# All three expert weights split in two, w_down multiplied by eighteen fp32r products: attention with a mixture of experts behind it, on one core

## The reference

```
x = layernorm(x + attn(x, bv_q, bv_k, bv_v))
    Q = sign(x * sign(bv_q)); K = sign(x * sign(bv_k)); V = x * sign(bv_v)
    attn = sum over s <= t of sigmoid(4 * Q.K / 16) * V        (causal)
x = layernorm(x + ffn(x, w_router, w_gate, w_up, w_down))
    top1 = argmax(softmax(x @ w_router)); 32 experts, 320 places each, in order of arrival
    g = buf @ w_gate[e]; u = buf @ w_up[e]                     (320 x 256, 256 x 256)
    y = (silu(g) * u) @ w_down[e]                              (320 x 256, 256 x 256)
    out = x + y * gate   for rows that got a place, else x
```

## Time and profile before

| | us |
|---|---|
| median of 3 runs | 582.45 |
| lowest, highest | 579.06, 582.63 |
| the profiled execution | 580.2 |
| its span | 578.5 |
| TensorE busy | 544.3 |
| VectorE busy | 386.5 |
| ScalarE busy | 356.0 |
| POOL busy | 380.7 |

### The profile page before, as it was taken

The page is one execution under the profiler, slowest core; times in us unless marked ns, Lnnn a source line. Parts: engine busy times, 40 slices in busy tenths (PEclk is TensorE's granted clock), DMA queues, the critical chain, the costliest instruction groups (busy, mean ns, idle before and its releaser), DMA issues.

```text
span 578.5 us, 11994 instructions
## 1 busy us (share of the span) xinstructions
PE 544.3 (94%) x3953; PEld 465.2 (80%) x3953; DVE 386.5 (67%) x986; ACT 356.0 (62%) x707; POOL 380.7 (66%) x547
## 2 busy tenths in 40 slices
PE   5999999999999999999998999999999999999960
PEld 4889898898888989889895388888888888888840
DVE  2765877957787669777664447667777777777730
ACT  5786977959778596877871135555555555555530
POOL 3547887688776878777753505666666666666663
PEclk9999999999999999999998899999999999999995
DMA  8994233243322443117410146666666666665300
GB/s 245 370 336 141 80 104 89 83 141 94 93 56 87 144 94 119 46 37 207 166 58 7 60 125 194 198 196 193 193 196 185 184 188 190 197 192 180 113 21 34
DMA packets 80637, 81.47 MB, mean 141 GB/s; under 512 B 20362, under 2 KB 71802, under 8 KB 80576
## 3 DMA queue, kind: packets, MB, share of 16 engines
q1 hardware_dynamic: 73664, 66.41, 38.9%
q0 software_dynamic: 6912, 14.30, 6.9%
HBM read 44.29 MB, written 37.90 MB: 142 GB/s over the span
## 4 chain that ended last, share of the span: by engine, by line
PE 84%; DVE 5%; issue 3%; DMA 2%; POOL 2%; ACT 1%; SPq 0%; DVEq 0%; POOLq 0%; ACTq 0%
PE ps L1004 15%; PE ps L838 10%; PE ps L839 10%; PE ps L840 10%; PE ps L816 9%; PE ps L982 8%; PE ps L990 6%; PE ps L983 6%; PE ps L960 2%; PE ps L857 2%; DVE hl_ring L1065 2%; PE ps L870 1%; DVE stats L1079 1%; DMA bv_row<-in_L_attn_bv_v_dram 1%; PE ps L965 1%
## 5 line engine op out<-in xcount | busy, mean ns | idle before, releaser
L838 PE MATMUL ps<-v_hl,hl_ring 128*128 128x256 f32 x544 | 176.2, 324 | 0.0
L839 PE MATMUL ps<-v_hl,hl_ring 128*128 128x256 f32 x544 | 153.4, 282 | 0.0
L840 PE MATMUL ps<-v_hl,hl_ring 128*128 128x256 f32 x544 | 153.1, 281 | 0.0
L568 POOL DMA_INDIRECT out_dram<-alone,ids x80 | 98.7, 1234 | 47.7 <-POOLq L546 27.0
L838 PEld LDWEIGHTS ps<-v_hl,hl_ring 128*128 128x128 f32 x544 | 103.3, 190 | 14.3
L839 PEld LDWEIGHTS ps<-v_hl,hl_ring 128*128 128x128 f32 x544 | 103.5, 190 | 2.5
L1065 DVE TENSOR_TENSOR hl_ring<-ps,hl_ring 128x512 fp32r<-128x512 f32 (+3 forms) x160 | 92.8, 600 | 16.0 <-ACT ps L648 13.2
L840 PEld LDWEIGHTS ps<-v_hl,hl_ring 128*128 128x128 f32 x544 | 103.1, 190 | 0.0
L646 ACT ACTIVATE hl_ring<-ps 128x512 fp32r<-128x512 f32 (+3 forms) x160 | 85.9, 537 | 26.5 <-PE ps L819 14.6
L1004 PE MATMUL ps<-xall,a_buf 128*128 128x256 f32 (+1 forms) x384 | 92.9, 384 | 1.0 <-DVE a_buf L1262 1.0
L755 ACT ACTIVATE a_buf<-ps 128x320 f32<-128x320 f32 x64 | 28.0, 437 | 102.3 <-PE ps L990 102.1
(11 more groups left out here) (130 smaller groups left out, 920.8 us busy)
## 6 DMA issues: line engine op xcount, KB each, us to landing
expert_rows<-xs SPq DMA_DIRECT2D x40, 258.0 KB, 4.4
xs<-expert_rows SPq DMA_DIRECT2D x32, 258.0 KB, 2.9
xall<-in_L_attn_x_dram SPq DMA_DIRECT2D x16, 512.0 KB, 4.7
out_dram<-alone SPq DMA_DIRECT2D x16, 512.0 KB, 3.1
xall<-in_L_ffn_w_gate_dram SPq DMA_DIRECT2D x32, 256.0 KB, 3.5
xall<-in_L_ffn_w_up_dram SPq DMA_DIRECT2D x32, 256.0 KB, 3.9
xall<-in_L_ffn_w_down_dram SPq DMA_DIRECT2D x32, 256.0 KB, 4.6
xs<-expert_rows SPq DMA_DIRECT2D x32, 64.5 KB, 3.2
```

Of the source, the lines that this page charges most:

```text
L568: g_.indirect_dma_start(out=out_rows, out_offset=bass.IndirectOffsetOnAxis(ap=ids[:, e % U, t:t + 1], axis=0), in_=o_s[:, p, t, :], in_off ...
L838: mm(o, ah, v_hl[:, 0, j, :], start=(j == 0 and i % 2 == 0), stop=False, skip_group_check=True)
L839: mm(o, ah, v_hl[:, 1, j, :], start=False, stop=False, skip_group_check=True)
L840: last = mm(o, al, v_hl[:, 0, j, :], start=False, stop=(j == GT * g + i), skip_group_check=True)
```

## The change

- `v_hl` grows from 16 to 18 blocks. In the expert stage it holds three slots (e % 3) of six blocks, and `high_weights` and `low_weights` split all 1536 columns: w_down's two blocks with the others. The wait of `high_weights` is now for down of e-3 (`y_done`), and in the last batch of attention for 36 finished steps (`OFF[3] + 2 * WK`, WK = 6).
- `hidden` writes the product back to u's place in PSUM. ScalarE's new `high_hidden` rounds it to fp32r in `act_r`, VectorE's new `low_hidden` subtracts to get the low part.
- `down` makes eighteen fp32r products of 256 columns, for each half f and each of three tiles: high x high, high x low, low x high, every one with 128 weight columns. The padding columns of `act_r` are zero, set at the start. It waits for low_hidden(e, 0) before the first nine and for low_hidden(e, 1) before the other nine; `gate_up` waits for low_hidden of the expert before in place of hidden.
- VectorE's order becomes hidden(e, 0), low_x(e+1), low_hidden(e, 0), low_weights(e+1), hidden(e, 1), combine(e-1), its statistics in one piece behind it, low_hidden(e, 1). ScalarE has high_hidden(e, 0) behind high_x(e+1) and high_hidden(e, 1) behind silu(e, 1).
- At the end POOL issues the two stores of expert 30 ahead of second_rstd of expert 31.

```diff
-        v_hl = sb("v_hl", [P, 2, T // P, D], F32R)
+        v_hl = sb("v_hl", [P, 2, 3 * 2 * (DC + DC // 2), D], F32R)
+        act_r = sb("act_r", [P, 2, FC, 2, CAP + CREST], F32R)
...
+        def pair_tile_cols(e, t):
+            if t == CFULL:
+                return (0, P) if e % 2 else (CFULL * P, CFULL * P + P)
+            lo = t * P + (e % 2) * P
+            return lo, lo + P
+        def own_cols(e):
+            return (e % 2) * CREST, (e % 2) * CREST + CAP
...  POOL
             store(RL, 1, tiles_of(1)[1:])
+            store(RL, 2, tiles_of(2))
             second_rstd(RL, 3)
-            store(RL, 2, tiles_of(2))
             store(RL, 3, tiles_of(3))
...  ScalarE
-                atleast(act, gu_done, FC * (e - 1))
-                atleast(act, wl_ready, e - 1)
-                s_.activation(w_h[:, p, :, :], raw[:, s, 0:4, :], ACT.Copy).then_inc(wh_ready, 1)
+                atleast(act, y_done, CT * (e - 2))
+                atleast(act, wl_ready, e - 2)
+                s_.activation(w_h[:, e % 3, :, :], raw[:, s, 0:WK, :], ACT.Copy).then_inc(wh_ready, 1)
...
-                        act.wait_ge(pv_done, (B - 1) * NS + OFF[3] + 2 * GT)
+                        act.wait_ge(pv_done, (B - 1) * NS + OFF[3] + 2 * WK)
                         high_weights(0, (k - NS + 4) // 2)
...
+            def high_hidden(R, n, f):
+                e, p = R * U + n, n % 2
+                lo, hi = own_cols(e)
+                act.wait_ge(hp_ready, FC * e + f + 1)
+                atleast(act, y_done, (e - 1) * CT)
+                s_.activation(act_r[:, p, f, 0, lo:hi], ps[:, 3 + 2 * f, 0:CAP], ACT.Copy).then_inc(hh_ready, 1)
...  TensorE
-                atleast(pe, h_ready, FC * (e - 1) + f + 1)
+                atleast(pe, hl_ready, FC * (e - 1) + f + 1)
...
+                for f in range(FC):
+                    pe.wait_ge(hl_ready, FC * e + f + 1)
+                    wh, wl = w_h[:, e % 3, 4 + f, :], w_l[:, e % 3, 4 + f, :]
+                    for t in range(CT):
+                        lo, hi = pair_tile_cols(e, t)
+                        o = ps[:, 6 + t // 2, (t % 2) * D:(t % 2 + 1) * D]
+                        new = f == 0 and (t == 0 or t == CFULL and p == 0)
+                        mm(o, act_r[:, p, f, 0, lo:hi], wh, start=new, stop=False, skip_group_check=True)
+                        mm(o, act_r[:, p, f, 0, lo:hi], wl, start=False, stop=False, skip_group_check=True)
+                        last = mm(o, act_r[:, p, f, 1, lo:hi], wh, start=False, stop=(f == FC - 1),
+                                  skip_group_check=True)
...  VectorE
-                v_.tensor_tensor(act_h[:, p, f, :], act_s[:, f, :], ps[:, 3 + 2 * f, 0:CAP], ALU.mult)\
-                    .then_inc(h_ready, 1)
+                up = ps[:, 3 + 2 * f, 0:CAP]
+                v_.tensor_tensor(up, act_s[:, f, :], up, ALU.mult).then_inc(hp_ready, 1)
+            def low_hidden(R, n, f):
+                e, p = R * U + n, n % 2
+                lo, hi = own_cols(e)
+                dve.wait_ge(hh_ready, FC * e + f + 1)
+                v_.tensor_tensor(act_r[:, p, f, 1, lo:hi], ps[:, 3 + 2 * f, 0:CAP],
+                                 act_r[:, p, f, 0, lo:hi].bitcast(F32), ALU.subtract).then_inc(hl_ready, 1)
...
                 hidden(R, n, 0)
                 if ahead:
                     low_x(R, n + 1)
+                low_hidden(R, n, 0)
                 if ahead and n >= 1:
                     low_weights(R, n + 1)
+                hidden(R, n, 1)
                 if n >= 1:
                     combine(R, n - 1)
-                hidden(R, n, 1)
+                if n >= 1:
+                    pair_statistics(R, n - 1)
+                low_hidden(R, n, 1)
```

More of the change, by code:

```diff
@@ L139, in bass_postln_attn_moe_kernel @@
         raw = xall[:, 0:6 * U, :].rearrange("p (s k) f -> p s k f", k=6)
-        w_h, w_l = (v_hl[:, n, 0:4 * 2, :].rearrange("p (s k) f -> p s k f", s=2) for n in range(2))
+        WK = 6
+        w_h, w_l = (v_hl[:, n, 0:WK * 3, :].rearrange("p (s k) f -> p s k f", s=3) for n in range(2))
         r_flat = hl_ring[:, :, :, :].rearrange("p a r t -> p (a r t)")
@@ L223, in bass_postln_attn_moe_kernel @@
         silu_ready = sem("silu_ready")
-        h_ready = sem("h_ready")
+        pad_ready = sem("pad_ready")
+        hp_ready = sem("hp_ready")
+        hh_ready = sem("hh_ready")
+        hl_ready = sem("hl_ready")
         gu_done = sem("gu_done")
@@ L771, in turn @@
                     high_x(R, n + 1)
+                high_hidden(R, n, 0)
                 if n >= 2:
@@ L774, in turn @@
                 silu(R, n, 1)
+                high_hidden(R, n, 1)
             high_x(0, 0)
@@ L979, in gate_up @@
                     for c in range(DC):
-                        wh = w_h[:, p, 2 * u + c, f * P:(f + 1) * P]
-                        wl = w_l[:, p, 2 * u + c, f * P:(f + 1) * P]
+                        wh = w_h[:, e % 3, 2 * u + c, f * P:(f + 1) * P]
+                        wl = w_l[:, e % 3, 2 * u + c, f * P:(f + 1) * P]
                         mm(o, wh, xh[:, c, :], start=(c == 0), stop=False)
@@ L995, in down @@
                 e, s, p = R * U + n, n % U, n % 2
-                pe.wait_ge(h_ready, FC * (e + 1))
-                pe.wait_ge(raw_in[s], 48 * (R + n // U + 1))
                 atleast(pe, z_step, tiles_to(e))
-                for t in range(CT):
-                    lo, hi = tile_cols(e, t)
-                    row = CREST if t == CFULL and p == 1 else 0
-                    o = ps[row:row + hi - lo, 6 + t // 2, (t % 2) * D:(t % 2 + 1) * D]
-                    for f in range(FC):
-                        last = mm(o, act_h[:, p, f, lo:hi], raw[:, s, 4 + f, :], start=(f == 0), stop=(f == FC - 1))
-                    last.then_inc(y_done, 1)
+                for f in range(FC):
[9 more added lines that the diff above has]
+                                  skip_group_check=True)
+                        if f == FC - 1:
+                            last.then_inc(y_done, 1)
             def turn(R, n, ahead=True):
@@ L1018, in _ @@
             pe.wait_ge(zmv_clear, 1)
+            pe.wait_ge(pad_ready, 2)
             turn_x(0, 0)
@@ L1037, in _ @@
             v_.memset(hot[:, 0, GT, :], 0.0).then_inc(seen_ready, 1)
+            v_.memset(act_r[:, 0, :, :, CAP:CAP + CREST].bitcast(F32), 0.0).then_inc(pad_ready, 1)
+            v_.memset(act_r[:, 1, :, :, 0:CREST].bitcast(F32), 0.0).then_inc(pad_ready, 1)
             dve.wait_ge(qksgn_ready, 1)
@@ L1283, in combine, with pair_statistics @@
                                             op0=ALU.mult, op1=ALU.add).then_inc(z_step, 1)
-                    if t > 0:
-                        z_statistics(e, t - 1, p)
-                z_statistics(e, tiles_of(e)[-1], p)
+            def pair_statistics(R, n):
+                e, p = R * U + n, n % 2
+                for t in tiles_of(e):
+                    z_statistics(e, t, p)
                 atleast(dve, zrs_ready, e - 1)
@@ L1311, in _ @@
             combine(RL, 3)
+            pair_statistics(RL, 3)
 _INS = ["L0_attn_x", "L0_attn_bv_q", "L0_attn_bv_k", "L0_attn_bv_v", "L0_ffn_w_router", "L0_ffn_w_gate",
```

13 lines of the change are left out of this document (4 added, 9 removed).

## The result

The changed kernel took 588.39 us (median of four runs, 586.16 to 595.33) against 581.22 for the kernel before beside it: a ratio of 1.0114, 95% interval 1.0076 to 1.0152. By that ratio it is slower by 6.6 us, where I had forecast 1.1 less. (The ratio leaves out the run of 595.33 us, which is a slow run; the other three are 586.16, 586.23 and 590.56.) The profiled execution took 586.16 (span 584.4), against 580.2 (span 578.5).

What follows compares the result with a forecast made beforehand. TensorE bound the kernel before; the new order adds waits for VectorE. Terms: -6.45 (pairs) + 0.5 + 0.2 + 3.2 (attention's end) + 1.4 (kernel's end) = -1.1 us, giving 581.3 us, range 566 to 595.

Steps and rivals of the forecast that it cites:

- The loads on SyncE's queue: Expert stage: weight loads keep their wait conditions and run four experts ahead, so they add nothing.
- Down's products at 0.119: TensorE, expert stage: eighteen fp32r products at 0.119 us each, so down takes 2.14 us instead of 2.93.
- low_weights 1.75, hidden in place 0.49, high_weights "some 1.5": Expert stage: low_weights 1.21 to 1.75 us, hidden unchanged by writing to PSUM, ScalarE's high_weights 1.05 to some 1.5.
- The walked pair, 13.56: Expert stage: two experts' turns take 13.56 us, 0.43 less than before; fifteen pairs give -6.45 us.
- The places of the waits: TensorE idle once per pair behind low_hidden, before down's other nine products, and once behind low_weights, before the next gate-and-up.
- The rival of TensorE as the bound: Expert stage: TensorE stays the bound, pair 12.41 us, kernel 563 us; chance 0.25 including halfway to it.
- The rival of VectorE's lost overlap: Long half, hidden to low_weights: 14 instructions lose 0.08 us overlap each, pair 14.68, 598 us; chance 0.15 full, 0.06 part.
- End of attention, +3.2: high_weights(0, 0) waits for 36 steps instead of 32, delaying sigmoids and the last residual addition: +3.2 us.
- End of the kernel, +1.4: From the last gate-and-up's end to the last store's end: 15.6 us instead of 14.2, so +1.4.
- moving the stores is worth nothing: Kernel's end: old and new store order both end 15.6 us after the last gate-and-up.
- ScalarE's norms, which I called thin: Long half: three normalisations end about T + 6.9, silu wanted at T + 6.97; later POOL rstd would lengthen the path.
- The forecast's chances: Whole kernel: over 1% faster 0.30, over 1% slower 0.25, the rest 0.45; 573 to 590 us had 0.50.

Runs made afterwards that it cites:

- the slow order: low_hidden(e,1) moved ahead of the statistics on VectorE, against the changed kernel with loads early and first wait at 30: ratio 1.0194 to the kernel before.

## Why the prediction was wrong

The step that failed is "The loads on SyncE's queue keep their conditions and run four experts ahead: nothing." Each condition was kept, and one of them, combine(e), was moved back by the change's own new instructions and order on VectorE, with three weight loads queued behind it. Priced at nothing, the step had ScalarE waiting 10.9 us for w_down in one execution and 6.1 in the next. In the second, and in the run with only the first wait at 30, POOL's last pass was held up in five turns besides; in the five runs with the loads early and VectorE's order as it is, it never was. I asked what is queued behind a waiting instruction for ScalarE and for VectorE, and not for SyncE. Shown by the run with the loads early: it takes 7.6 us off and changes nothing but SyncE's queue. The time lies inside my range of 566 to 595, but it moved the other way.

The other steps, in their order:
- Down's products at 0.119: right. In the changed kernel they start 0.12 apart. The Trainium skill's 109 ns ("TensorE: Matmul & The Clock Gate", Back-to-back issue gap), which I had set beside it, is given there as the gap of an isolated product.
- low_weights 1.75, hidden in place 0.49, high_weights "some 1.5": measured 1.75, 0.49 to 0.50 and 1.49.
- The walked pair, 13.56: right as soon as the loads don't hold it (13.5). That the sum comes out as well (-1.1 forecast, -1.4 between the spans of that run's profile and the one before) is luck in part: the stage gave 6.8 instead of 5.75, and the end of the kernel took 1.0 more than its price. In the changed kernel the pair is about 14.0 in one execution and 14.4 in the other.
- The places of the waits: right for low_weights (the row of 13.0 us above). Before down's second half it is smaller than the 0.56 I walked: 0.6 us in three waits on PE's own list in the changed kernel, and with the loads early 0.3 in a pair from start to start (453.54 to 453.97 instead of 0.12).
- The rival of TensorE as the bound, 563 us: it came about in no version with low_weights in one instruction. With it in two, TensorE is busy for 191 of 195 us of the stage (first busy column of this table row), and the pair is 13.1, still 0.7 over the 12.4 I gave that rival. 0.5 of it is the wait for low_hidden between down's halves (462.30 to 463.04 for two products instead of 0.24); the rest is not traced. The table row:

```profile
345.00:540.00 195.00, 191.25 (x1400) 186.92 (x1399) 185.58 (x430) 145.12 (x251) 126.16 (x230) 1.00 0.61 189
```

- The rival of VectorE's lost overlap: fell. Instructions in a row still overlap by 0.08 and 0.09 (453.54 + 1.75 against 455.20, 455.60 + 1.26 against 456.78). The section of the Trainium skill that I had named for it ("VectorE: DVE Perf Modes", The DRAIN you can't avoid) says as well that a next instruction that is not held starts earlier, and that is what these rows show.
- End of attention, +3.2: right. It is 3.1 in both executions and 3.1 by undoing the wait, and ScalarE's idle 5.37 is as forecast. The other 2.0 in the first execution lie ahead of it.
- End of the kernel, +1.4: measured +2.4. (My 15.6 was to the last store's end, which came at 16.5; the 15.6 of the table is to its start.) The mis-sized term is rstd's start to the first store. I took 2.22 from the earlier trace rows, where stores stood between them and covered the norm; moved ahead, they cover nothing, and it is 3.15. So "moving the stores is worth nothing" was wrong by 0.9, shown by moving them back.
- ScalarE's norms, which I called thin ("If POOL's rstd came later, the excess would go onto the path"): that is what the rows show where POOL's pass is held up. ScalarE waits for rstd 7.2 us in all in the first execution of the changed kernel, 22.8 in the second, 42.2 in the slow order (not all of it costs time: it is 10.5 with the loads early, where no pass is long). I had written the condition down and given it no price and no chance.

The forecast's chances had no case for a late DMA. Its ways to be slower all lay on engines.

## What to carry to other kernels

When an instruction is moved back on one engine, list every queue that waits for it, the DMA queue too, and for each transfer behind that wait work out the time from release to landing against the time at which it is wanted; a distance counted in iterations is not a time. Where one queue carries loads with different conditions, try the one that is free earliest first: here that was worth 1.3%. Price a wait on a pipelined engine from start to start, not by the idle time in its row, and a fixed latency only from a row with the same instructions in between.

## What the runs showed of the hardware

A VectorE tensor_tensor with both inputs in SBUF (low_weights, 1.75 us) holds up a POOL instruction that starts behind it (or, by the records, up to 0.03 us ahead) until it ends. A POOL pass of 3 elements a partition takes 1.69 instead of 0.20, another 2.32 instead of 0.89. With low_weights cut to a first part of 1.2 us, a copy of 0.18 takes 1.18. In the slow order all fourteen long passes end 0.04 to 0.06 us after low_weights. A POOL instruction that is already running when low_weights starts keeps its length (0.89 from 444.42 in the second execution of the changed kernel, low_weights from 445.27). The row of VectorE's key scaling at the kernel's head (1.61 instead of 0.35) looks like the same in the other direction, beside a POOL product of 2.35 that started first; no run was made for it. The Trainium skill, "SBUF — State Buffer" (Who interferes with whom), says that a VectorE instruction with two SBUF inputs and a GpSimd instruction that reads SBUF contend, that the shared pair of ports is an exclusive lock, and that the order of issue decides who blocks. The trace agrees with it to 0.05 us (low_weights ends at 453.48, the pass at 453.53). I had not used it: a change that makes such an instruction longer by 0.54 us also makes POOL's worst case longer by that, and whether it is met depends on a phase of 0.1 us: pass at 451.84 and low_weights at 451.73 in the slow order, POOL's last copy at 455.35 and low_weights at 455.50 with the loads early, where nothing is held up.
